# Attention and quantised FFN on one core: the first two batches share the first stage, and GpSimd issues the loads of contexts and of x

## The reference

```python
def reference(x, ctx, w_gate, w_up, w_down):
    q, k, v = heads(layernorm(x)), heads(ctx), heads(ctx)
    attn = softmax(einsum('bhqd,bhkd->bhqk', q, k) / sqrt(16))
    x = x + einsum('bhqk,bhkd->bhqd', attn, v)
    z = quant(layernorm(x))                       # fp4 grid, blocks of 16
    h = silu(z @ quant(w_gate).T) * (z @ quant(w_up).T)
    return x + quant(h) @ quant(w_down).T         # inner width 704
```

## Time and profile before

| | us |
|---|---|
| median of 3 runs | 539.81 |
| lowest and highest of them | 536.22, 544.4 |
| the profiled execution | 537.67 |
| span of its profile | 535.8 |
| busy in the span: PE, DVE, ACT, POOL | 486.7, 437.2, 370.5, 293.5 |

### The profile page before, as it was taken

One profiled execution on the slowest core, in us unless ns is written; L12 is line 12 of the kernel. 1 busy time (PEld: TensorE's weight loads), 2 busy tenths in 40 slices (PEclk: granted clock), 3 DMA queues, 4 the chain that ended last, 5 costly groups with the idle time before them and its releaser, 6 DMA issues.

```text
span 535.8 us, 13755 instructions
## 1 busy us (share of the span) xinstructions
PE 486.7 (91%) x4036; PEld 382.7 (71%) x4036; DVE 437.2 (82%) x1127; ACT 370.5 (69%) x739; POOL 293.5 (55%) x423
## 2 busy tenths in 40 slices
PE   1558999999999999999767799999999999999996
PEld 0224555566666666655445799999999999999996
DVE  1566889999999999988444889888899888898764
ACT  3426989999999999977663465666655665566653
POOL 5323555566565565534415566666666667666543
PEclk9957999999999999999887899999999999999999
DMA  7989666666666666420000000000000000000000
GB/s 205 252 180 289 170 178 175 182 186 185 186 185 188 197 197 196 115 65 2 3 0 2 0 16 17 20 20 20 16 14 20 20 20 20 10 19 21 21 21 31
DMA packets 50457, 49.03 MB, mean 92 GB/s; under 512 B 5241, under 2 KB 48121, under 8 KB 50425
## 3 DMA queue, kind: packets, MB, share of 16 engines
q1 hardware_dynamic: 50424, 48.65, 32.7%
HBM read 18.94 MB, written 4.19 MB: 43 GB/s over the span
## 4 chain that ended last, share of the span: by engine, by line
PE 73%; DVE 6%; POOL 5%; issue 5%; SPq 5%; DMA 3%; ACT 2%; POOLq 0%; DVEq 0%; ACTq 0%
PE SC L1101 21%; PE PV L1101 12%; PE PV L1055 9%; PE MX L1037 9%; PE SC L1023 8%; PE T L1126 4%; SPq L296 4%; DVE MF L731 3%; DMA QS<-MT 3%; PE T L1131 2%; PE T L1006 2%; PE SC L1126 1%; PE T L974 1%; PE T L981 1%; PE MX L1069 1%
## 5 line engine op out<-in xcount | busy, mean ns | idle before, releaser
L731 DVE TENSOR_REDUCE MF<-MX 128x2 f32<-128x512 f32 x256 | 165.8, 683 | 28.5 <-PE MX L1037 25.0
L575 ACT ACTIVATE P<-SC 128x512 f32<-128x512 f32 x256 | 140.3, 593 | 27.4 <-PE SC L1023 25.8
L1037 PE MATMUL MX<-KS,QS 96*128 96x256 bf16 x512 | 102.9, 285 | 6.1 <-DVE MF L731 4.3
L1023 PE MATMUL SC<-QS,KS 98*128 98x256 bf16 x512 | 100.2, 278 | 8.0 <-DMA QS<-MT 8.0
L498 POOL TENSOR_TENSOR HQ<-HN,hscale 128x704 f32<-128x704 f32 x31 | 43.2, 1392 | 60.5 <-DVE HN L865 60.5
L1023 PEld LDWEIGHTS SC<-QS,KS 98*128 98x128 bf16 x512 | 44.0, 99 | 40.9 <-ACT P L575 19.1
L663 ACT ACTIVATE HH<-T 128x768 fp32r<-128x768 f32 x31 | 25.2, 813 | 65.8 <-PE T L1126 65.8
L1055 PE MATMUL PV<-P,VA 128*32 128x256 f32 x1024 | 69.8, 391 | 0.5 <-ACT OT L584 0.5
L1101 PE MATMUL SC<-WH,XH 128*128 128x352 f32 x256 | 68.2, 348 | 0.0
L1037 PEld LDWEIGHTS MX<-KS,QS 96*128 96x128 bf16 x512 | 43.7, 100 | 33.9 <-DVE MF L731 25.0
L1101 PE MATMUL SC<-WH,XL 128*128 128x352 f32 x256 | 62.9, 327 | 0.0
(11 more groups left out here) (134 smaller groups left out, 1027.3 us busy)
## 6 DMA issues: line engine op xcount, KB each, us to landing
KS<-KP SPq DMA_DIRECT2D x96, 128.0 KB, 3.0
QS<-QP SPq DMA_DIRECT2D x96, 128.0 KB, 2.5
QN<-in_x_p SPq DMA_DIRECT2D x16, 256.0 KB, 2.9
KT<-in_ctx_t SPq DMA_DIRECT2D x16, 256.0 KB, 3.0
C<-in_ctx SPq DMA_DIRECT2D x16, 256.0 KB, 3.7
X<-in_x SPq DMA_DIRECT2D x16, 256.0 KB, 4.5
out<-OB SPq DMA_DIRECT2D x32, 128.0 KB, 1.7
W<-in_L_ffn_w_down SPq DMA_DIRECT2D x1, 704.0 KB, 7.0
```

The lines of the kernel that those rows point to most:

```text
L575: nc.scalar.activation(P[g % 2][:, j, :, :], SC[h % 3][:, :, :], ACT.Exp, scale=0.25).then_inc(exp_done, 1)
L731: nc.vector.tensor_reduce(MF[st.slot(off, 2)][:, :, h:h + 1], MX[h % 2][:, :, :], AX.X, ALU.max, negate=True).then_inc(mx_done, 1)
L1023: last = nc.tensor.matmul(SC[h % 3][:, k, :], KS[r][0:ROWS, h, k * 128:(k + 1) * 128], QS[r][0:ROWS, h, :], start=True, stop=True)
L1037: last = nc.tensor.matmul(MX[h % 2][:, q, :], QS[r][0:PROD, h, q * 128:(q + 1) * 128], KS[r][0:PROD, h, :], start=True, stop=True)
```

## The change

- Contexts C and rows X of x are no longer loaded by SP (`load_second` is gone) but by `nc.gpsimd.dma_start` at the head of POOL's step: C of batch t+2 and x of batch t+1, before the additions. Each kind of load has a semaphore of its own.
- Step -3 on ACT, DVE and PE becomes `first_steps`, which prepares batches 0 and 1 together; step -2 has nothing left for ACT, and for PE the third part of the queries. DVE makes the first KR, which POOL made before.
- SP: the DMAs of keys and queries of batches 0 and 1 come one after the other; the load of w_gate moves behind them, that of w_up and w_down from step -1 to the end of step 0, `load_first(3, 3)` behind the DMA of MT. The four DMAs of ones go from SP to ACT.
- Steps before 0: PE transposes the maxima and ACT copies them one piece of the queries earlier; DVE does the weights' first pieces at place (3, 3). DVE waits for w_up and w_down in step 2, no longer in step 1.

```diff
@@ SP
-            def load_second(b, r):
-                sp.dma_start(C[r][:, :, :], c_d[:, bass.ds(b * QT, QT), :]).then_inc(loaded[r], 16)
-                sp.dma_start(X1[:, tiles(b)].rearrange("p (q c) -> p q c", q=QT),
-                             x_d[:, bass.ds(b * QT, QT), :]).then_inc(loaded[r], 16)
...
             load_first(0, 0)
             load_first(1, 1)
+            first_keys(0)
+            first_queries(0)
+            load_first(2, 2)
+            first_keys(1)
+            first_queries(1)
             sp.wait_ge(w_zeroed, 4)
             load_square(0, wg_in)
-            first_stack()
-            load_first(2, 2)
-            for b in range(2):
-                load_second(b, b)
...
                     load_first(st.item(RING), st.slot(RING, RING))
-                    load_second(st.item(RING), st.slot(RING, RING))
...
+                if st.first == -1:
+                    load_first(3, 3)
                 if st.has(LEAD):
                     sp.wait_ge(q_out, st.times(LEAD, 3, 3))
                     gate(sp)
                     stack(QS[r_q(st)], QP[st.slot(LEAD, 2)], (0, 0, 0, 1, 1, 2), r_q(st))
-                    if st.first == 1 - LEAD:
-                        load_ones()
-                        load_second(2, 2)
-                        load_first(3, 3)
-                    if st.first == 2 - LEAD:
-                        load_second(3, 3)
-                        load_rest()
+                if st.first == 0:
+                    load_rest()
@@ POOL
+            def load_context(b, r):
+                nc.gpsimd.dma_start(C[r][:, :, :], c_d[:, bass.ds(b * QT, QT), :]).then_inc(c_loaded[r], 16)
+
+            def load_x(b, r):
+                nc.gpsimd.dma_start(X1[:, tiles(b)].rearrange("p (q c) -> p q c", q=QT),
+                             x_d[:, bass.ds(b * QT, QT), :]).then_inc(x_loaded[r], 16)
+
             def attention_step(st):
+                if st.first == 1 - LEAD:
+                    load_context(0, 0)
+                if st.first >= -1 and st.has(2):
+                    load_context(st.item(2), st.slot(2, RING))
+                if st.first >= -1 and st.has(1):
+                    load_x(st.item(1), st.slot(1, RING))
                 if st.has(-2):
+                    pool.wait_ge(x_loaded[st.slot(-2, RING)], st.turn(-2, RING, 16))
                     for q in range(QT):
...
-                if st.has(LEAD):
+                if st.has(LEAD) and st.first > -LEAD:
@@ ACT
+            def first_steps(st, nx):
+
                 key_part(st, 0)
                 key_part(st, 1)
                 for q in range(QT):
                     normalise(st, q)
+                key_part(nx, 0)
+                part_out(QP[0], TB, 0, q_tr, q_out, st)
+                key_part(nx, 1)
+                part_out(QP[0], TB, 1, q_tr, q_out, st)
+                part_out(QP[0], TB, 2, q_tr, q_out, st)
+                for q in range(QT):
+                    normalise(nx, q)
                 for n in range(3):
+                    part_out(QP[1], TB, n, q_tr, q_out, nx)
+                act.wait_ge(ones_ready, 1)
+                for r in range(RING):
+                    nc.scalar.dma_start(KS[r][PROD:ROWS, :, :].rearrange("d h t -> d (h t)"), ones[:, :]).then_inc(ones_out, 16)
@@ DVE
+            def first_steps(st, nx):
+
+                statistics(st)
+                aggregate(st)
+                dve.wait_ge(k_out, 1)
+                nc.vector.tensor_tensor(KR[:, :], KT[0][:, :], KP[0][:, 0, :], ALU.subtract).then_inc(k_rest, 1)
+                statistics(nx)
+                aggregate(nx)
@@ PE
+            def first_steps(st, nx):
                 for n in range(3):
                     queries(st, n)
+                for n in range(2):
+                    queries(nx, n)
```

More of the change, by code:

```diff
@@ L197, in program @@
         HP = T[:, :, :].rearrange("p a (b c) -> p (a b) c", c=128)[:, 0:NT, :]
[L199 removed]
+        x_loaded, kt_loaded, qn_loaded, c_loaded = ([sem(f"{n}{r}") for r in range(RING)] for n in
+                                                    ("x_loaded", "kt_loaded", "qn_loaded", "c_loaded"))
         stacked = [sem(f"stacked{r}") for r in range(RING)]
@@ L303, in load_square @@
                 sp.dma_start(WN[m][0:FI - full * 128, full, :], w[full * 128:FI, :]).then_inc(w_loaded[m], 16)
-            def load_ones():
-                sp.wait_ge(ones_ready, 1)
-                for r in range(RING):
-                    sp.dma_start(KS[r][PROD:ROWS, :, :].rearrange("d h t -> d (h t)"), ones[:, :]).then_inc(ones_out, 16)
             def load_rest():
@@ L613, in attention_step @@
                                 normalise(st, q)
+                        if (g, j) == (2, 3) and st.first < 0:
+                            maxima_out(st)
                         for n, at in enumerate(((2, 0), (2, 3), (3, 3))):
@@ L616, in attention_step @@
                                 part_out(QP[st.slot(LEAD, 2)], TB, n, q_tr, q_out, st)
-                        if (g, j) == (2, 3) and st.has(1):
+                        if (g, j) == (2, 3) and st.first >= 0 and st.has(1):
                             maxima_out(st)
@@ L788, in weight_maxima @@
                     dve.wait_ge(w_loaded[0], 32)
-                elif st.first == 1:
+                elif st.first == 2:
                     dve.wait_ge(w_loaded[1], 32)
@@ L815, in attention_step @@
                         maximum(st, g, j)
-                        if (g, j) == (0, 3) and st.has(LEAD):
+                        if (g, j) == (0, 3) and st.has(LEAD) and st.first > 1 - LEAD:
                             statistics(st)
                             aggregate(st)
-                        if (g, j) == (1, 1) and st.has(SCALE):
+                        if (g, j) == ((1, 1) if st.first >= 0 else (3, 3)) and st.has(SCALE):
                             weight_maxima(st)
@@ L828, in attention_step @@
                             round_weights(st)
-                        if (g, j) == (3, 0) and st.has(SCALE):
+                        if (g, j) == ((3, 0) if st.first >= 0 else (3, 3)) and st.has(SCALE):
                             weight_limits(st)
@@ L833, in attention_step @@
                             output(st, 1)
-                        if (g, j) == (3, 2) and st.has(SCALE):
+                        if (g, j) == ((3, 2) if st.first >= 0 else (3, 3)) and st.has(SCALE):
                             weight_inverses(st)
@@ L1083, in attention_step @@
                         max_scores(st, g, j)
+                        if (g, j) == (2, 3) and st.first < 0 and st.has(1):
+                            maxima(st)
                         for n, at in enumerate(((2, 1), (2, 3), (3, 1))):
-                            if (g, j) == at and st.has(LEAD):
+                            if (g, j) == at and st.has(LEAD) and (n == 2 or st.first > 1 - LEAD):
                                 queries(st, n)
-                        if (g, j) == (2, 3) and st.has(1):
+                        if (g, j) == (2, 3) and st.first >= 0 and st.has(1):
                             maxima(st)
```

50 lines of the change are left out of this document (29 added, 21 removed).

## The result

The changed kernel takes 548.51 us, median of 4 runs (545.47 to 550.86), beside 539.59 of the kernel before (4 runs on the same chip). The ratio is 1.0182, 95% interval 1.014 to 1.0225: slower by 1.8%, with an interval that holds 2% inside it, so whether it is slower by 2% stays unclear. The prediction was 540.6, with a range from 531.5 to 551.0. The time lies in the range, near its slow end, and outside the likeliest case's own 536 to 546.

A forecast was written before the change was run, and what follows sets the result against it. The prediction took PE to bound the steps and waits for transfers the start-up. Start-up -5.6 (-6.6 + 1.0) plus 6.4 for POOL's issues gave +0.8, so 538.5 profiled and 540.6 as median; range 531.5 to 551.

The forecast's parts named there:

- likeliest case: Whole kernel: an issue on POOL costs 0.6 to 1.0 us, total 536 to 546 us; chance 0.42.
- The price of an issue on POOL: Head of POOL's step: each load issue holds POOL for d = 0.8 us, between 0.39 and 1.16.
- The cost of a step: Steps 3 to 13: two issues delay KR, ACT and PE; a step loses 2d - 1.0 = 0.6 us, eleven 6.4.
- the slack: Later steps, between POOL, DVE, ACT and PE: 1.0 us of the two issues' time is absorbed before a step lengthens.
- The start-up's -6.6: Before step 0: earlier reductions and a freer SP queue bring the first scores from 41.90 to 35.3, ends 5 and 8.
- The landing: Before step 0: the maxima's DMA lands after 3.2 us instead of 5.47.
- the ones on ACT's queue, four issues of some 0.65: First stage, 20.6 to 23.2: they delay batch 2's first key part without cost; uncovered, up to 2.6 us.
- What comes back: Step 1: w_up and w_down, moved there, cost 1 us, ends 0 and 2.
- The issues are hidden: Rival for POOL's issues in the steps: they cost nothing, only the start-up's gain is left, 534 us; chance 0.27.
- POOL becomes the bound: Rival for steps 3 to 13: ACT waits for KR; at d = 1.16 the sum is +8.9, 549 us; chance 0.21.
- The start-up is bound by the DMA engines: Rival for the start-up: bytes, not order, bind it; about half of the 6.6 us comes, 544 us; chance 0.10.
- within 2%: Total: differs from the kernel before by less than 2%, between 529 and 550.6 us; chance 0.80.

The follow-up runs named there:

- e9_behind: Changed kernel with POOL loading C and X only for batches 0 to 3, SP later ones behind the maxima's DMA; w_up, w_down after steps 1, 2: 539.11 us.
- e2_sp: Changed kernel with all loads of C and X back on SP's queue, the new first stage kept: 545.03 us, ratio 1.0063 to the kernel before.
- e1_later: Changed kernel with POOL's two load issues moved within its step, behind KP and VA, before its weights' passes: 553.52 us, ratio 1.0246 to the kernel before.
- e5_ones: Changed kernel with the four DMAs of ones issued by SP ahead of batch 2's keys, not by ACT: 548.39 us, ratio 1.0163 to the kernel before.
- e6_weights: Changed kernel with w_up loaded at the end of SP's step 1 and w_down at the end of step 2: 547.33 us, ratio 1.0123 to the kernel before.
- e8_mt: Changed kernel with ones on SP, C and X on SP (from batch 4 behind the maxima's DMA), w_up and w_down after steps 1 and 2: 539.69 us.
- e12b_late: e9_behind with x of batch t loaded by SP behind the maxima of step t, C of batch 4 one step later: 534.33 us, ratio 0.9877 to the kernel before.
- e7_pool_only: Kernel before with only the loads of C and X moved to POOL, of batch t+3 in each step: 548.45 us, ratio 1.0161 to the kernel before.

## Why the prediction was right, and where it was wrong

The total was in the range, and the sum behind it was not good: +0.8 us was forecast for the profiled execution, and its span is 8.0 longer. (The sum has a slip: eleven steps of 0.6 are 6.6, not 6.4.) By its steps:

**The price of an issue on POOL** was right. I took d = 0.8 from a row of another pass, between 0.39 and 1.16; the rows give 0.82 and 0.72, mean 0.77. The estimate from the Trainium skill ("DMA: Bandwidth & Descriptors", section "Latency and other measured facts"), d = 1.0, was too high: that section's 1 us is a time to the first byte, not the issuing engine's time.

**The cost of a step** was too small, 0.6 for a measured 0.76. The mechanism was as written: KR late, ACT's second key part late, PE late. The mis-sized term is the slack. I subtracted 1.0 us: POOL's 0.43, the 0.4 by which DVE would bring winv forward, and PE's 0.2. Three holds give 0.74 to 0.80. The 0.4 did not come: POOL still waits 0.59 us for winv (0.58 before), and KR ends 5.07 us after the first scores instead of 3.97, later by 1.10, which is the 1.54 less the 0.43 alone. The other 0.3 or so lies between ACT and PE. Eleven steps make 8.4 instead of 6.4, 2 us of the error. That taking C and X off SP brings the later steps nothing was right. e9_behind shows it: SP issues them behind the maxima's DMA there, POOL issues none in the late steps, and such a step takes 14.14 (14.15 before, 14.16 in e2_sp, both with them ahead of the keys). The Trainium skill's rule that issuers share the same DMA engines ("DMA: Bandwidth & Descriptors", section "Issuing engines are not separate DMA queues") agrees with it; its remark that the saved issue time is usually small does not decide here: what POOL spends does, 1.54 us a step.

**The start-up's -6.6** came as -3.3. The landing was better than I took it (2.41 for 3.2), and the issue of the maxima's DMA was wrong: 36.13 for 32.1. In the prediction's terms "the ones on ACT's queue, four issues of some 0.65" failed: they took 6.14. I had named this cover and its price if gone, 2.6 us, and took it to hold; KP of batch 2 then ended at 32.03, not 27.9. The reductions began at 18.55, not 17.5, since the queries' DMAs landed after 4.38 us and not 2.5 to 3. Behind both lies a term that the prediction put at nothing: C of batch 1 and X of batch 0, which the change itself issues on POOL at 13.14 and 13.97. With these two moved (e1_later) the reductions begin at 16.83, the ones take 4.17, and the maxima's DMA goes at 32.44, near the forecast 32.1; in e2_sp it goes at 32.25. But then the landing is 4.53 and 7.05 us. So the order was worked out well, and no version had both the early issue and a short landing. e5_ones shows the same: with the ones off ACT the landing takes 3.8 us.

**What comes back** was put at +1.0, between 0 and 2. Steps 1 and 2 give back 3.77, less 0.75 gained in step 0. I had looked only at the maxima's DMA. The queries' DMAs are late too (6.13), and the granted clock is 0.88 in step 2, behind the wait. So the start-up in sum is -0.3 and not -5.6; this is the larger error, 5.3 us.

**The rivals.** "The issues are hidden" fell. "POOL becomes the bound" is right in its place, ACT's wait for KR, and its total of 549 is near the measured one, but by another sum: it had 14.5 from the steps and -5.6 from the start, and the runs show 8.4 and -0.3. "The start-up is bound by the DMA engines", with a chance of 0.10, is what e1_later, e5_ones, e6_weights, e8_mt, e9_behind and e12b_late bear out. Its "about half of the 6.6" is the measured 3.3 at step 0 by number only: the maxima's DMA landed fast, and the bytes acted earlier, on the queries' DMAs and the ones. It missed that steps 1 and 2 take the other half. This rival and the cost on POOL held at once, and I had treated them as alternatives. The chance of 0.80 on "within 2%" was given for sums that did not happen; that 1.8% still falls into it is luck in part.

## What to carry to other kernels

A DMA issued by a compute engine is an instruction of that engine: count its hold against the slack of the next thing that is waited for, and take one idle gap of the trace for one gap, not several added up. A gap in an engine's time is not free either when the transfer then runs beside a small DMA on the critical path; ask of each load what lands next to it, and move it to where it is first needed, not to where a queue happens to be idle. When an order is changed to bring one wait forward, list every wait of the same stretch: the versions of this start-up gave back most of what they had gained, and the one that kept it had loads moved out of the stretch and not only reordered in it.

## What the runs showed of the hardware

- An issue by GpSimd of 128x2x256 float32 (256 rows of 1 KB) took 0.82 or 0.72 us of the engine's own time in the steps, one of 128 rows 0.59.
- Four small DMAs (2x64x64 each) took 4.0 to 4.3 us to issue on ACT's queue where GpSimd had issued no load some 7 us earlier, and 5.5 to 7.3 where it had. On SP's queue they took 2.35 (e7_pool_only), 3.08 (before), 4.04 (e8_mt) and 5.17 (e5_ones). Most issues of a load of 256 KB took 0.3 to 0.8 us in SP's queue; a few took up to 1.74.
- The 16 KB of the maxima landed in 2.3 to 2.5 us when no load was just ahead, in 2.8 to 5.2 behind or beside a few, and in 5.47 (before), 7.05 (e2_sp) and 7.08 (e8_mt) behind four loads of 256 KB.
- Moving 512 KB from ahead of the keys' DMAs or behind the maxima's (late step 14.14 or 14.15) to just ahead of the maxima's made the step 16.18 us, the bytes and the engine being the same.
